# Attention probabilities transposed as 32x32 blocks on VectorE and regrouped through DRAM, with new engine orders, in a two-layer graph attention kernel

## The reference

```python
# layer 0, adj as mask and as edge attribute
nx = ln(x, ln1_g, ln1_b)
q, k, v = heads(nx @ wq + bq), heads(nx @ wk + bk), heads(nx @ wv + bv)
bias = where(adj > 0, 0.1 * adj * adj, -inf)
attn = softmax(q @ k.T / sqrt(32) + bias)
x1 = x + (merge(attn @ v) @ wo + bo)
x2 = x1 + gelu(ln(x1, ln2_g, ln2_b) @ w1 + b1) @ w2 + b2
# layer 1
w = softmax(where(adj == 0, -inf, (x2 @ Wq) @ (x2 @ Wk).T / 16))
out = ln(x2 + (w @ (x2 @ Wv)) @ Wo + bo1, gamma, beta)
```

## Time and profile before

| what | us |
|---|---|
| median of three runs (914.96 to 917.57) | 915.56 |
| profiled execution: its span, first to last instruction | 913.2 |
| what the median has beyond that span | 2.4 |
| TensorE busy | 892.7 (98%) |
| VectorE busy | 693.0 (76%) |
| ScalarE busy | 638.4 (70%) |
| GpSimd busy | 389.6 (43%) |
| DMA: 26.29 MB in 29743 packets, share of the span of 16 engines | 9.1% |

### The profile page before, as it was taken

How to read it: one execution, slowest core, us unless ns; L and a number is a source line. 1 busy time by engine, 2 the same in 40 slices (tenths; PEclk the granted TensorE clock), 3 DMA queues, 4 the chain that set the end, 5 groups by cost and what they waited for, 6 DMA issues and landing times.

```text
span 913.2 us, 22669 instructions
## 1 busy us (share of the span) xinstructions
PE 892.7 (98%) x7623; PEld 808.4 (89%) x7623; DVE 693.0 (76%) x2580; ACT 638.4 (70%) x1888; POOL 389.6 (43%) x258
## 2 busy tenths in 40 slices
PE   8989999999999999999999999999999999999996
PEld 7878898989989898998989989898998989898795
DVE  7786868779696877959778695877969687786736
ACT  5784958768495876949577694866859587684842
POOL 4633243635516354352645425363551536444222
PEclk9999999999999999999999999999999999999998
DMA  8101000100101010000100101010010100000001
GB/s 266 36 1 36 1 24 25 37 24 23 34 0 34 23 34 23 14 24 19 34 23 23 34 0 34 23 34 23 23 34 0 34 23 29 11 24 2 1 24 35
DMA packets 29743, 26.29 MB, mean 29 GB/s; under 512 B 1142, under 2 KB 29452, under 8 KB 29708
## 3 DMA queue, kind: packets, MB, share of 16 engines
q1 hardware_dynamic: 29692, 25.83, 9.1%
q10 hardware_dynamic: 16, 0.00, 0.0%
HBM read 17.44 MB, written 8.39 MB: 28 GB/s over the span
## 4 chain that ended last, share of the span: by engine, by line
PE 87%; DVE 4%; ACT 4%; issue 3%; POOL 1%; POOLq 0%; DVEq 0%; ACTq 0%
PE bank L364 22%; PE bank L366 21%; PE bank L365 21%; PE bank L521 5%; PE bank L513 3%; PE bank L532 3%; PE bank L634 3%; PE bank L659 3%; ACT bank L934 2%; PE bank L615 2%; PE bank L554 1%; PE bank L458 1%; PE bank L652 1%; DVE p_s L1296 1%; ACT bank L965 1%
## 5 line engine op out<-in xcount | busy, mean ns | idle before, releaser
L934 ACT ACTIVATE bank<-p_s,neg_max 128x128 f32<-128x128 f32 x512 | 181.7, 355 | 11.1 <-DVE neg_max L1296 11.0
L1707 POOL TENSOR_TENSOR rstd<-ve,minus_half 128x4 f32<-128x4 f32 (+1 forms) x49 | 54.2, 1106 | 300.5 <-DVE ve L1259 300.5
L364 PE MATMUL bank<-w_hi,hT_hi 128*128 128x256 f32 x512 | 147.4, 288 | 0.0
L366 PE MATMUL bank<-w_hi,hT_lo 128*128 128x256 f32 x512 | 144.1, 281 | 0.0
L365 PE MATMUL bank<-w_lo,hT_hi 128*128 128x256 f32 x512 | 144.1, 281 | 0.0
L1296 DVE CUSTOM_DVE_ANT_0 p_s<-bank,bias 128x128 f32<-128x128 f32 x512 | 112.9, 288 | 3.2 <-PE bank L513 3.2
L1190 DVE TENSOR_TENSOR hT_lo<-bank,hT_hi 128x512 fp32r<-128x512 f32 (+1 forms) x151 | 95.7, 657 | 19.2 <-ACT hT_hi L877 19.0
L364 PE MATMUL bank<-n2T_hi,w_hi 128*128 128x512 f32 (+1 forms) x272 | 108.3, 398 | 0.5 <-DVE hT_lo L1190 0.5
L366 PE MATMUL bank<-n2T_hi,w_lo 128*128 128x512 f32 (+1 forms) x272 | 103.8, 382 | 0.0
L365 PE MATMUL bank<-n2T_lo,w_hi 128*128 128x512 f32 (+1 forms) x272 | 103.7, 381 | 0.0
L364 PEld LDWEIGHTS bank<-w_hi,hT_hi 128*128 128x128 f32 x512 | 96.4, 188 | 2.7 <-DVE hT_lo L1190 1.2
(11 more groups left out here) (228 smaller groups left out, 2441.4 us busy)
## 6 DMA issues: line engine op xcount, KB each, us to landing
xs<-in_x SPq DMA_DIRECT2D x15, 512.0 KB, 3.8
out<-y SPq DMA_DIRECT2D x14, 512.0 KB, 3.0
adj_i<-in_adj SPq DMA_DIRECT2D x15, 256.0 KB, 2.8
out<-y SPq DMA_DIRECT2D x3, 256.0 KB, 2.2
x2T_f<-in_L_gnn_w SPq DMA_DIRECT2D x1, 512.0 KB, 6.6
tT<-in_L_gnn_w SPq DMA_DIRECT2D x1, 512.0 KB, 8.2
y<-in_L_gnn_w SPq DMA_DIRECT2D x1, 512.0 KB, 6.4
vo<-in_L_gnn_w SPq DMA_DIRECT2D x1, 512.0 KB, 8.3
```

Of the source, the lines that this page charges most:

```text
L364: mm(out, a_hi, b_hi, start=first, stop=False)
L366: return mm(out, a_lo, b_hi, start=False, stop=last)
L934: last = run(bank[r][:, NODES * place:NODES * place + NODES], p_s[:, r, place, :], ACT.Exp, scale=-1.0, bias=neg_max[:, r, place:place + 1 ...
L1707: P.tensor_tensor(t["rstd"][:, 0:k], t["ve"][:, 0:k], minus_half[:, 0:k], ALU.pow).then_inc(ln_pool[n], 1)
```

## The change

From group 2 on, the probabilities of a pair are not transposed on TensorE. VectorE transposes them in SBUF as blocks of 32x32 (`blocks`, one `STREAM_TRANSPOSE` per r, `p_s` to `pT`); for this the 128 columns of a place are cut into four column blocks b, and block b of partition block a lands transposed in partition block a. What is left is a move between partitions: SP stores the four partition blocks of `pT` into a DRAM tensor `parked` (`store_blocks`, four DMAs, runs of 512 bytes) and loads it back with the key as partition (`load_blocks`, runs of 2 KB), the first pair to `pT`, the second to `p_s`. `attend` waits for that load and reads its operand as four runs of 32 columns (`pT_part`). `p_transpose` and `pT_copy` remain for groups 0 and 1 alone.

All of a group's attention is moved: both pairs of gp now have scores, exponents, division and blocks in the turn in which gp is the newest, and `attend` follows in the next turn, for both pairs side by side. The orders of all engines are written anew for that, the banks are reassigned (`usual_banks`, `first_banks`), and the `lo` and `hi` parts of the second pair's attention result lie in `n2T` instead of `hT`. `first_turn` gets the second pair of group 2 as well.

```diff
+        parked = nc.dram_tensor("parked", (2, HPT, NODES // 32, 32, NODES // 32, NODES), f32).ap()
...
+        def by_blocks(g):
+
+            return not (isinstance(g, int) and g < 2)
+
+        def pT_part(g, q, r, place):
+            t = pT_of[q]
+            return t[:, r, :, 32 * place:32 * place + 32] if by_blocks(g) else t[:, r, place, :]
...
+            def store_blocks(g, q):
+                sp.wait_ge(dve_blocks, blocks_done(g, q, HPT - 1))
+                for a in range(NODES // 32):
+                    sp.dma_start(parked[q].rearrange("r b j a x -> j (r b) a x")[:, :, a, :],
+                                 pT[32 * a:32 * a + 32, :, :, :].rearrange("p r b x -> p (r b) x")).then_inc(park_store[q], 16)
+
+            def load_blocks(g, q):
+                for u in pairs(g):
+                    sp.wait_ge(park_store[u], 64 * g - 64)
+                sp.dma_start(pT_of[q][:, :, :, :].rearrange("p r a x -> p r (a x)"),
+                             parked[q].rearrange("r b j a x -> (b j) r (a x)")).then_inc(park_load[q], 16)
...
+            def turn(gp, ga, gc):
+                store_blocks(ga, 1)
+                load_blocks(ga, 0)
+                load_blocks(ga, 1)
+                if not is_last(gp):
+                    load_adj(gp + 1)
+                store(gc)
+                store_blocks(gp, 0)
+                if not is_last(gp):
+                    load_x(gp + 1)
...
+                elif m == 0:
+                    pe.wait_ge(dve_nxT, 2 * g + 2)
...
+                if by_blocks(g):
+                    if q == 1:
+                        pe.wait_ge(dve_p, 4 * pair0(g) + 4)
...
+                if by_blocks(g):
+                    pe.wait_ge(park_load[q], 16 * g - 16)
...
             def turn(gp, ga, gb):
+                for j in range(6):
+                    mlp_up(gb, j, True)
+                norm_transpose(gp)
+                mlp_up(gb, 6, True)
+                mlp_up(gb, 7, True)
+                project_k(gp, 0)
+                project_k(gp, 1)
+                project_q(gp, 0)
+                project_q(gp, 1)
+                mlp_down(gb, 0, (0,))
+                attend(ga, 0)
+                attend(ga, 1)
+                scores(gp, 0)
+                mlp_down(gb, 0, (1,))
+                mlp_down(gb, 1)
+                if size(gp) > 2:
+                    scores(gp, 1)
+                x2_transpose(gb)
+                out_project(ga, 0)
+                out_project(ga, 1)
+                t_project(gb)
+                project_v(gp, 0)
+                scores1(gb, True)
+                vo_project(gb, 0, True)
+                vo_project(gb, 1, True)
+                n2_transpose(ga, True)
+                p1_transpose(gb)
+                if size(gp) > 2:
+                    project_v(gp, 1)
...
+            def blocks(g, q, r):
+                dve.wait_ge(dve_p, 4 * (pair0(g) + q) + r + 1)
+                if r == 0:
+                    if q == 0:
+                        dve.wait_ge(pe_av, pair0(g) - 1)
+                    else:
+                        dve.wait_ge(park_store[0], 64 * g - 64)
+                V.transpose(pT[:, r, :, :].rearrange("p b (l i) -> p l b i", l=4),
+                            p_s[:, r, :, :].rearrange("p l (b j) -> p l b j", j=32)).then_inc(dve_blocks, 1)
...
             def turn(gp, ga, gb, gc):
+                whole = size(gp) > 2
+                sums1(gp)
+                moments(1, gp)
+                h_low(gb, 0)
+                sums3(gc)
+                norm1(gp)
+                h_low(gb, 1)
+                h_low(gb, 2)
+                moments(3, gc)
+                h_low(gb, 3)
+                norm3(gc)
+                h_low(gb, 4)
+                nxT_low(gp)
+                for j in range(5, HT):
+                    h_low(gb, j)
+                for r in range(HPT):
+                    biased(gp, 0, r)
+                attn_low(ga, 0)
+                divided(gp, 0, 0)
+                blocks(gp, 0, 0)
...
+                residual2(gb, 1)
+                blocks(gp, 0, 3)
+                if whole:
+                    biased(gp, 1, 0)
+                    biased(gp, 1, 1)
+                x2T_low(gb)
+                residual1(ga, 0, True)
+                if whole:
+                    biased(gp, 1, 2)
+                residual1(ga, 1, True)
+                if whole:
+                    biased(gp, 1, 3)
+                sums2(ga, 0)
+                sums2(ga, 1)
+                moments(2, ga)
+                t_copy(gb)
+                if whole:
+                    divided(gp, 1, 0)
+                    blocks(gp, 1, 0)
+                norm2(ga)
+                biased1(gb)
+                if whole:
+                    divided(gp, 1, 1)
+                    blocks(gp, 1, 1)
+                vo_copy(gb)
+                if whole:
+                    divided(gp, 1, 2)
+                    blocks(gp, 1, 2)
+                n2T_low(ga)
+                inverse_sums1(gb)
+                if whole:
+                    divided(gp, 1, 3)
+                    blocks(gp, 1, 3)
+                residual3(gb, 0)
+                residual3(gb, 1)
```

More of the change, by code:

```diff
@@ L334, in _ @@
                 load_row(dst, src, row_load)
[L335 to L346, removed]
+            load_adj(2)
+            load_x(2)
+            store_blocks(2, 0)
+            load_adj(3)
+            load_x(3)
+            def turn(gp, ga, gc):
[8 more added lines that the diff above has]
+                    load_x(gp + 1)
+            turn(3, 2, 0)
+            with sp.Fori(3, GROUPS - 3) as g:
+                turn(g + 1, g, g - 2)
+            turn(GROUPS - 2, GROUPS - 3, GROUPS - 5)
+            turn(GROUPS - 1, GROUPS - 2, GROUPS - 4)
+            load_blocks(GROUPS - 1, 0)
+            store(GROUPS - 3)
             for q in range(2):
@@ L582, in mlp_up, with mlp_down @@
                 last.then_inc(pe_up, 1)
-            def mlp_down(g, q):
-                if q == 0:
+            def mlp_down(g, q, graphs=(0, 1)):
+                if q == 0 and graphs[0] == 0:
                     pe.wait_ge(dve_h, HT * g + (7 if isinstance(g, int) and g == 0 else 5))
-                for b in (2 * q, 2 * q + 1):
+                for b in [2 * q + i for i in graphs]:
                     for i in range(HT):
@@ L593, in mlp_down @@
                                    i == 0, i == HT - 1)
[L594 removed]
+                if graphs[-1] == 1:
+                    last.then_inc(pe_down, 1)
             def last_down(g, b, tiles):
@@ L1464, in turn @@
-                if A:
-                    pT_copy(ga, 0, 3)
-                if B:
-                    h_low(gb, 3)
-                if P:
-                    sums1(gp)
-                    moments(1, gp)
-                if C:
-                    norm3(gc)
-                if B:
-                    for j in range(4, HT):
-                        h_low(gb, j)
-                if A2:
-                    biased(ga, 1, 0)
-                if P:
-                    norm1(gp)
-                if A2:
-                    biased(ga, 1, 1)
-                    biased(ga, 1, 2)
-                    biased(ga, 1, 3)
-                    divided(ga, 1, 0)
@@ L1500, in turn @@
-                if B:
-                    x2T_low(gb)
-                if A2:
-                    residual1(ga, 0, B)
-                    sums2(ga, 0)
-                    residual1(ga, 1, B)
-                if A2:
-                    sums2(ga, 1)
-                    moments(2, ga)
-                if B:
-                    t_copy(gb)
-                if A and B:
-                    norm2(ga)
-                if A:
-                    n2T_low(ga)
-                if B:
-                    biased1(gb)
@@ L1517, in turn @@
-                if P:
-                    biased(gp, 0, 0)
-                    biased(gp, 0, 1)
-                    biased(gp, 0, 2)
-                if B and size(gb) > 2:
-                    vo_copy(gb)
-                if P:
-                    biased(gp, 0, 3)
-                if B:
-                    inverse_sums1(gb)
-                if P:
-                    divided(gp, 0, 0)
-                if B:
-                    for q in pairs(gb):
-                        residual3(gb, q)
@@ new lines, in turn @@
+                nxT_low(gp)
+                for j in range(5, HT):
+                    h_low(gb, j)
+                for r in range(HPT):
+                    biased(gp, 0, r)
+                attn_low(ga, 0)
+                divided(gp, 0, 0)
+                blocks(gp, 0, 0)
+                divided(gp, 0, 1)
+                blocks(gp, 0, 1)
+                residual2(gb, 0)
+                divided(gp, 0, 2)
+                divided(gp, 0, 3)
+                attn_low(ga, 1)
+                blocks(gp, 0, 2)
```

414 lines of the change are left out of this document (150 added, 264 removed).

## The result

| | us |
|---|---|
| before, median of 4 runs (914.96 to 917.57) | 915.51 |
| changed, median of 4 runs (958.16 to 960.60) | 959.84 |
| ratio, 95% interval | 1.0476 [1.0459, 1.0492] |
| profiled span before, changed | 913.2, 957.8 |

The kernel became 4.8% slower. First the page of the changed kernel: span, busy times, TensorE's clock in 40 slices, shares of the chain that ended last, two groups of VectorE (busy, mean ns | idle time before, and what ended it) and the DMA issues (count, KB each, us to landing).

The account below looks back on a forecast made before the run. TensorE bound the old 54.15 us turn; new waits make 57.2. First turn +18.5, thirteen turns +39.7, turn 16 -4.0, last -1.75: +52.4 on 913.2 gives 965.6, plus 2.4 is 968 us; range 942 to 1012.

Parts of the forecast that it names:

- Step (1): VectorE's head of a turn, 0 to 6.0 us after its last residual3; TensorE goes on with the sixth mlp_up at 6.2.
- Step (2): TensorE from the sixth mlp_up to the scores, 6.2 to 23.3 us; project_k waits half a microsecond for nxT_low.
- Step (3): VectorE from the scores to the end of residual3: 33.9 us, with eight block transposes at 0.61 each.
- Ends: First turn +18.5 us, turn 16 -4.0, last turn -1.75.
- The way through DRAM: Stores 7.5 us and loads 6.0 per pair, second load 4.4 more: hidden; rival, data late: 1020 to 1072 us, chance 0.08.
- TensorE stays the bound: Rival: the ring takes under 50.65 us, so TensorE's work sets the turn; 875 us, chance 0.11.
- the ring: Chain of waits in a turn: VectorE's head, TensorE up to the scores, VectorE's rest; 23.3 + 33.9 = 57.2 us.
- The signs: If right: turn 56 to 59 us, TensorE below 90% busy with three waits, VectorE idle some 9 us before first biased.
- one sign of being wrong: Listed as showing the forecast wrong: TensorE or VectorE released by the DMA of parked.
- Blocks cheap or dear: Rivals on VectorE's block transposes: cheap, no change, chance 0.04; dear, 1.15 us each, 1025 us, chance 0.08.
- The break-even of 0.23 us: VectorE block transposes at 0.23 us each, 0.38 less than taken, would leave the turn unchanged.
- The clock: TensorE's clock should stay at granted 1.00, with TensorE waiting 6.5 us in a turn.

Follow-up runs that it names:

- Experiment 2: Changed kernel with sums3, moments3 and norm3 moved behind VectorE's last h_low (GpSimd's rstd(3) behind its bias): 936.97 us, ratio 1.0225.
- experiment 4: Changed kernel without the stores to and loads from the DRAM buffer, attend waiting for its group's last blocks instead: 956.42 us, ratio 1.0456.
- Experiment 5: Changed kernel with each block transposition of VectorE issued twice, the second waiting for the first: 1043.89 us, ratio 1.1388.
- experiment 3: Changed kernel with the new orders of experiment 1 and Experiment 2 together: 905.88 us, ratio 0.9891.
- experiment 6: Changed kernel with each block transposition covering only the first 32 of 512 columns, all waits and transfers kept: 920.89 us, ratio 1.0047.
- experiment 1: Changed kernel with TensorE's first graph of mlp_down(gb, 0) moved behind scores(gp, 0): 934.63 us, ratio 1.0203.
- experiment 7: experiment 3's kernel with VectorE's t_copy ahead of sums2's second half and biased1 ahead of norm2: 897.97 us, ratio 0.9817.

## Why the prediction was right

968 us were forecast, 959.84 came; the sign, the cause and the place were right.

- *Step (1)*: the sixth `mlp_up` at 6.2 us. It started at 457.19, 6.08 behind `residual3`, after a wait of 1.10 for `h_low`.
- *Step (2)*: `project_k` at 11.8, scores done at 23.3. Measured 463.14, that is 12.03, after 0.63 for `nxT_low`, and 23.65; VectorE idle 10.3 where "over 9" was written. Experiment 2 took the last norm (`sums3`, `moments`, `norm3`) out of the way of this step and gained 2.3 a turn.
- *Step (3)*: 33.9 forecast, 56.46 - 23.65 = 32.8 measured. This is the mis-sized term. A block is spaced 0.64, not 0.61 (+0.24 for eight); but a block behind its quotient is spaced 0.72 (422.93 to 423.65), not the 0.84 of `residual1` before `sums2`, 0.6 less over the six; and the waits of 0.45 and 0.4 for `x2_transpose` and `vo_project` were some 0.3 together, 0.55 less. That is 0.9 of the 1.1. So a turn grew by 2.32 instead of 3.05, 13 x 0.73 = 9.5 us less; with the ends, 1.65 more (next point), these are the 7.8 us by which the forecast span, 965.6, was too long.
- *Ends*: first turn +19.5 (forecast 18.5), with 1.1 in it of a block that waits for the first stores, which the forecast had not; nor had it the lower clock there (0.80 from 84.00 to 112.56), so that the two numbers come so close is in part luck. Turn 16 and the end -5.1 (-5.75).
- *The way through DRAM*: the last of a pair's four stores landed and the load was issued 6.2 us behind the first store, where 7.5 was taken; loads 5.5 and 7.7 (6.0, and 10.4 for the second from its issue). Hidden, as experiment 4 shows by itself.
- *TensorE stays the bound*: no. Experiment 5 adds VectorE time alone and nearly all of it arrives at the end. Only with the ring cut by 4 us (experiment 3) do turns come near TensorE's work, 51.0 us where the prediction subtracted its way to 50.65. Over the changed kernel TensorE's busy time fell by 28.8 us and not by the 50.8 of the transposes: a turn at clock 1.00 has 51.68 of 54.15 left, which is 2.5 less where 3.50 were taken.
- *The signs*: a turn of 56 to 59 us, the three waits of TensorE and the one of VectorE came as written. "TensorE below 90% busy" did not: it is 90.2% of the span, and in a turn at clock 1.00 it idles 4.7 us, not 6.5. And one sign of being wrong did show, small and once: VectorE released by the stores of `parked`, after 1.1 us, in the first turn.
- *Blocks cheap or dear*: 0.71 us long. The break-even of 0.23 us start to start that the prediction gave was not measured; with small blocks (0.21 long, 0.13 start to start) a turn is 53.86 against 54.15, just on the other side of it. The Trainium skill (VectorE: DVE Perf Modes, section "The three transpose paths") gives 311 ns for a 128x128 bf16 square on VectorE, as an estimate 1.24 us for the four squares of a block. The row shows 0.708 for four squares in f32; the measurement decides. Two rows suggest why the estimate is too long: 0.708 for 512 columns and 0.210 for 32 (experiment 6) make, as an estimate, 0.18 us for an instruction and 1.04 ns for each column, so 0.31 for the 128 columns of one square, and four squares in one instruction pay the 0.18 once.
- *The clock*, which "should stay" at 1.00, did not. The end of the first turn and the start of turn 3 ran at 0.69 (window 100.00 to 122.20), and one of the twelve turns counted, the one in the window 475.14 to 531.60, at 0.97, 0.6 us dearer (`residual3` to `residual3` 56.99). The growth of a turn does not come from it, as the eleven turns at 1.00 take 56.43. What it costs at the start was not separated.

The Trainium skill (Perfetto Trace Analysis, section "Identifying the Most-Contended Engine") names the engine with the highest occupancy as the one to optimise first, and for TensorE MFU (its arithmetic as a share of the peak) and the busy share of the weight loads as the better measures. The change did just that: it took 28.8 us off TensorE, the fullest by its matmuls and by its weight loads, and lost 44. On the changed kernel the rule points to TensorE again (90%, weight loads 80%) and not to VectorE (76%), though the 82 us of work that experiment 5 gave VectorE (806.8 busy for 725.0) made the time 84 us longer. The Trainium skill (Perfetto Trace Analysis, section "Optimization Strategy") has one look for the gaps on the engine and for what blocks it there, and make that start sooner. Experiments 1 to 3 agree, with turns of 56.48 brought down to 52.42.

## What to carry to other kernels

Work moved off the fullest engine pays only if the engine that takes it has its free time where the work falls: follow one turn as a ring, from what an engine waits for to who waits for it, and add up the ring, not the engines. Where one engine idles long at one place of each turn, what stands ahead of that place in its queue and is not needed there belongs behind it, and work of the engine it waits for belongs behind the result. The same instructions then ran in 898 us instead of 960.

## What was not expected of the hardware

- A block transposition of VectorE over 128x512 f32 cost little more than a copy out of a bank: 0.708 us against 0.682, though it gathers 32-column pieces; one behind the other, the second waiting for the first, they are spaced 0.74.
- TensorE's clock fell in some turns and not in others of the same instructions: in experiment 2 six of twelve ran at 0.97, each 0.57 us longer, in the changed kernel one of twelve, in experiment 5 all twelve at 0.97 or 0.95; in experiments 1, 3, 4, 6 and 7 all twelve stood at 1.00. How long TensorE idles does not decide it by itself: at 1.00 it was 3.1 us a turn in experiment 1 (54.70 less 51.59 busy) and 4.6 in experiment 4 (56.35 less 51.75), against 3.0 in the turns at 1.00 of experiment 2. The 0.71 of a stretch of 4.5 us is a mixture of the two levels, 1.2 and 2.4 GHz. Why the clock fell in one turn and not in the next stays open.
- The way through DRAM, 87.11 - 26.29 = 60.8 MB of stores and loads, hardly touched the rest: the turn was 0.13 us shorter without it, or 0.08 if the changed kernel's one turn at clock 0.97 is left out.
